# The second turn of x in an even unit: spread at step 5, turned ahead of step 8, copied at step 10

## The reference

```python
e = stack([tbl_f[ids[:, f]] for f in range(39)], axis=1)             # (2048, 39, 16)
z0 = einsum('bid,bjd->bdij', e, e).reshape(B, D, 39 * 39)
cur0 = relu(einsum('bdk,kl->bld', z0, W0))                           # (B, 128, 16)
next_h, direct0 = split(cur0, 2, axis=1)
z1 = einsum('bid,bjd->bdij', e, next_h).reshape(B, D, 39 * 64)
cur1 = relu(einsum('bdk,kl->bld', z1, W1))
z = sum(concatenate([direct0, cur1], axis=1), axis=-1)
h = relu(concatenate([z, dense_ctx], axis=1) @ W_top1 + b_top1)
y = relu(h @ W_top2 + b_top2) @ W_top3
```

## Time and profile before

| | |
|---|---|
| median of 3 runs | 1513.18 us (1512.98 to 1514.53) |
| profiled execution | 1513.26 us |
| its span, first to last instruction | 1511.5 us |
| PE busy | 1442.2 us (95%) |
| DVE busy | 1384.0 us (92%) |
| ACT busy | 822.5 us (54%) |
| POOL busy | 971.7 us (64%) |

### The profile page before, as it was taken

One profiled execution on the slowest core, in us unless ns is written; L12 is line 12 of the kernel. 1 busy time (PEld: TensorE's weight loads), 2 busy tenths in 40 slices (PEclk: granted clock), 3 DMA queues, 4 the chain that ended last, 5 costly groups with the idle time before them and its releaser, 6 DMA issues.

```text
span 1511.5 us, 14915 instructions
## 1 busy us (share of the span) xinstructions
PE 1442.2 (95%) x4458; PEld 785.7 (52%) x4458; DVE 1384.0 (92%) x1244; ACT 822.5 (54%) x897; POOL 971.7 (64%) x604
## 2 busy tenths in 40 slices
PE   4888999999999999999999999999999999999999
PEld 3444545555555554555555555555555555545556
DVE  6778999999999999998999999999999989999993
ACT  1535655655456555545665654556565555655555
POOL 7888888888888778686877868686886830000000
PEclk8999999999999999999999999999999999999999
DMA  5867779888787888877788887878898786778610
GB/s 150 200 154 199 203 190 214 211 186 209 188 205 188 213 198 202 211 184 197 193 199 203 212 204 181 207 190 197 201 207 209 181 207 192 191 194 202 174 35 1
DMA packets 130717, 282.67 MB, mean 187 GB/s; under 512 B 36468, under 2 KB 61700, under 8 KB 130508
## 3 DMA queue, kind: packets, MB, share of 16 engines
q1 hardware_dynamic: 96070, 268.06, 70.4%
q0 software_dynamic: 19200, 4.95, 3.1%
q10 hardware_dynamic: 15366, 8.70, 2.3%
HBM read 273.67 MB, written 7.87 MB: 186 GB/s over the span
## 4 chain that ended last, share of the span: by engine, by line
PE 51%; DVE 26%; issue 14%; POOL 4%; ACT 3%; ACTq 2%; DVEq 0%; DMA 0%
PE psB L533 22%; DVE z L953 12%; PE psA L533 9%; DVE z_lo L962 8%; DVE z_split L953 6%; PE psB L570 4%; PE psB L563 4%; POOL emb L512 4%; PE psB L566 3%; ACTq L751 2%; PE psB L541 1%; ACT z_hi L816 1%; PE psA L553 1%; DVE feat_c L1018 1%; PE psA L563 1%
## 5 line engine op out<-in xcount | busy, mean ns | idle before, releaser
L512 POOL DMA_INDIRECT emb<-in_tbl,ids_all x600 | 971.5, 1619 | 254.5 <-issue 180.1
L533 PE MATMUL psB<-z,w 128*128 128x512 f32 x1544 | 694.0, 594 | 4.1 <-DVE z L953 4.1
L816 ACT ACTIVATE z_hi<-z_split 128x1024 fp32r<-128x1024 f32 x286 | 300.4, 1057 | 465.6 <-DVE z_split L953 410.0
L533 PEld LDWEIGHTS psB<-z,w 128*128 128x128 f32 x1544 | 292.2, 190 | 355.1 <-issue 331.6
L953 DVE TENSOR_TENSOR z<-h_quad,x_lay 128x1024 f32<-128x1024 f32 x354 | 420.2, 1216 | 9.9 <-PE psB L533 4.1
L962 DVE TENSOR_TENSOR z_lo<-z_split,z_hi 128x1024 fp32r<-128x1024 f32 x286 | 349.4, 1222 | 57.7 <-ACT z_hi L816 56.5
L953 DVE TENSOR_TENSOR z_split<-h_quad,x_lay 128x1024 f32<-128x1024 f32 x222 | 267.5, 1217 | 1.7 <-ACT h_quad L769 1.7
L769 ACT ACTIVATE h_quad<-psA 32x1024 f32<-32x1024 f32 x248 | 251.4, 1014 | 3.7
L533 PE MATMUL psA<-z,w 128*128 128x512 f32 x512 | 240.4, 592 | 0.7 <-DVE z L953 0.7
L563 PE MATMUL psB<-z_hi,w_hi 128*128 128x512 f32 x444 | 156.6, 434 | 18.0 <-ACT z_hi L816 18.0
L570 PE MATMUL psB<-z_lo,w_hi 128*128 128x512 f32 x444 | 144.6, 407 | 19.1 <-DVE z_lo L962 17.2
(11 more groups left out here) (121 smaller groups left out, 836.7 us busy)
## 6 DMA issues: line engine op xcount, KB each, us to landing
x_lay<-x_rows SPq DMA_DIRECT2D x1152, 128.0 KB, 7.0
bases<-x_rows SPq DMA_DIRECT2D x62, 468.0 KB
x_more<-x_rows SPq DMA_DIRECT2D x62, 468.0 KB
x_lay<-x_rows SPq DMA_DIRECT2D x64, 256.0 KB, 3.9
x_ring<-x_rows SPq DMA_DIRECT2D x31, 468.0 KB
emb<-in_tbl,ids_all POOLq DMA_INDIRECT x600
x_last<-x_rows SPq DMA_DIRECT2D x64, 128.0 KB, 9.7
x_rows<-x_side ACTq DMA_DIRECT2D x58, 120.0 KB
```

Source lines behind the costliest of these rows:

```text
L512: nc.gpsimd.indirect_dma_start(emb[t % 2][:, f * D:(f + 1) * D], None, tables[f], bass.IndirectOffsetOnAxis(ids_all[:, t, f:f + 1], 0)).th ...
L533: mm = nc.tensor.matmul(ps[:, cs], w[0:k, :], z[WHOLE_NO[place] % NZ][0:k, cs], start=first, stop=last)
L816: nc.scalar.activation(z_hi[n % NS][0:k, 0:cols], z_split[n % NS][0:k, 0:cols], ACT.Copy).then_inc(z_hi_made, 1)
```

## The change

For u = 2, 4, ..., 28 the turn of unit u+3 on PE goes from ahead of step 11 to ahead of step 8. ACT's spread of an odd unit goes from one step ahead of the turn to three, its copy stays two steps behind it: spread at step 5 (was 10), copy and stores at step 10 (were at 13). In the body of u = 0 the turn of unit 3 stays ahead of step 15 and its copy at step 17; its spread goes from step 14 to 12. The first turn of each even body (unit u+2: spread at 0, turn ahead of 2, copy at 4) stays as it is.

```diff
@@ def turns(u):
     if u % 2 or u + 2 >= UNITS:
         return ()
-    return ((u + 2, 9), (u + 3, 15)) if u == 0 else ((u + 2, 2), (u + 3, 11))
+    return ((u + 2, 9), (u + 3, 15)) if u == 0 else ((u + 2, 2), (u + 3, 8))
@@ ACT's body(u)
                 for s in range(STEPS1):
                     for v, t in turns(u):
-                        if s == t - (2 if v % 2 == 0 else 1):
+                        if s == t - (2 if v % 2 == 0 else 3):
                             spread_x(v)
                         if s == t + 2:
                             keep_x(v)
```

## The result

| | before | after |
|---|---|---|
| median | 1513.54 us (1512.98 to 1514.53, 4 runs) | 1469.45 us (1468.99 to 1469.76, 4 runs) |
| ratio | | 0.9708 (95% interval 0.9691 to 0.9725) |
| span of the profiled execution | 1511.5 us | 1467.9 us |

The change makes the kernel 44.1 us faster, 2.9%. The forecast was 1470.6.

What follows compares the result with a forecast made beforehand. PE and DVE, both nearly full and coupled, were taken to bound the kernel, with PE setting the pace. 14 x (2.15 + 0.67 + 0.22) = 42.6 us off 1513.2 gave 1470.6 us, range 1468 to 1484.

Steps and rivals of the forecast that it cites:

- The bottleneck and the stall's cause: PE and DVE nearly full; in even bodies ACT's copy at step 13 awaits PE's turn, delaying `high(13)`: DVE idle 3.15 us.
- 2.15 us for the even body: Half step 12 to splits 13 and 14: PE took 6.09 us, against 3.94 in the odd body; difference 2.15 us gained.
- 0.67 and 0.22 us for the odd body: PE's waits for `z_lo` at step 9 (0.67 us) and step 3 (0.22 us) should both go, through DVE's new lead.
- The thin margins: Odd body: DVE's 1.00 us of new lead exceeds the 0.89 us of waits by 0.11; `z` ring at step 1 leaves 0.14.
- a reserve of 0.11 us in DVE's lead: Odd body: DVE's new lead of 1.00 us against 0.89 us of PE's waits for `z_lo`, 0.11 us to spare.
- the ring: Full `z` buffers at step 1 of the odd body could hold DVE; margin 1.14 us before, 0.14 after: just fits.
- rival 1: Only the even body's stall goes, DVE's lead being lost on the way: 14 x 2.15 = 30.1 us gained, 1483.1 us; 22%.
- The costs taken as nothing: Even body: spread at step 5 (2.2 us cover), turn before step 8 (net 0.01 us), copy at 10 (3.1 us cover): 0.
- Rival 2: A new DVE wait, for `x_lay` or `z_hi` elsewhere, partly replaces the old: 1498 us, range 1488 to 1508; 8%.
- Rival 3: Slower: DMA becomes the bound, stores and gathers delaying SP's loads; at 8 us later, 27 us slower, 1540 us; 4%.
- the reserve of 3.1 us: Step 2 of the odd unit: time left between the `x_lay` load's landing and its use in the new kernel, 3.1 us.
- Rival 4: The change doesn't do what it says: the late `high(13)` has another cause than the copy; 1513 us; 4%.

Runs made afterwards that it cites:

- the full dose: Changed kernel with DVE's product of step 16 done a second time (1024 columns) in the 14 even bodies, into an unread tile: 1485.63 us.

## Why the prediction was right

**The bottleneck and the stall's cause** held as told. The prediction read from rows 3 to 5 that ACT had room on average and none at step 13. Moving the turn (with the spread that it needs) brings all of the gain and moving the spread alone none, so the cause is where the prediction put it: PE's late turn, handed on through ACT's order.

**2.15 us for the even body.** From step 15 of the odd body before it to its own step 15 PE took 723.41 - 679.24 = 44.17 us and takes 703.31 - 661.34 = 41.97: 2.20. Right.

**0.67 and 0.22 us for the odd body.** From there to step 15 of the next odd body PE took 766.73 - 723.41 = 43.32 and takes 745.65 - 703.31 = 42.34: 0.98, where 0.89 was forecast. The sum of a pair was 3.04, its size in the trace 87.50 - 84.31 = 3.19. The term that was somewhat too small is the price of a wait. The next two starts of PE after the waits in rows 6, in the kernel before:

```profile
741.61 1.88 PE L533 MATMUL psA<-z,w 128*128 128x512 f32 x4
...
756.48 1.88 PE L533 MATMUL psA<-z,w 128*128 128x512 f32 x4
```

After 741.03 and 755.90 they come 0.58 us later, where a part without a wait in front takes 0.46: a wait costs PE its gap and some 0.12 us more. Two such waits are 0.24; in the other direction, step 9 still loses 0.57 - 0.46 = 0.11 in the changed kernel, and as much again behind it (735.44 - 734.87 = 0.57). Together 0.89 + 0.24 - 0.22 = 0.91 of the 0.98.

**The thin margins** (a reserve of 0.11 us in DVE's lead, and 0.14 us at the ring) are the point at which rival 1 would have won. That the forecast came out so near is in part luck: the sum left out the price behind each wait (0.24 us too little) and the small wait that stays (0.22 us too much), and the two nearly cancel. The first margin was too hopeful by about 0.2 us: the 0.57 us at 734.87 is a small wait where none was forecast. A wait of that size costs 0.22 us, not the whole term.

**The costs taken as nothing** were nothing. Spread and `relu1` end before `high(7)` with 2.3 us to spare (2.2 forecast); the copy's stores with 2.9 (3.1 forecast). The turn at its new place takes 691.89 - 690.99 = 0.90 together with the split part behind it, the same 0.90 that its neighbour before step 2 took the earlier trace rows. An estimate from the 275 ns that the Trainium skill (TensorE: Matmul & The Clock Gate, Part 4) gives for a transpose, four of them taken serially, would have made it 1.1 us more than the split part; the trace decides for 0.44.

**The rivals.** Rival 1 (1483) is excluded by the measured time and by PE's waits for `z_lo`, 17.2 us before and 0.6 after. The runs with more work on DVE show that the term it leaves out is real: the full dose brings the waits at steps 3 and 9 back and costs 1.16 us a pair, near the 0.89 + 0.24 = 1.13 above. Rival 2 (a new wait in part) isn't in the changed kernel, but it is what happens when the copy is moved instead of the turn: 1487 us. Rival 3 (DMA) didn't come, and the runs with more traffic show how far off it was: with three times 448 KB a body DVE waited for `x_lay` 3.2 us in the whole span. The expectation of 100 us had assumed that 1344 KB make the loads 6.5 us later; they were issued 2.6 us later and took no longer in the median, and the reserve of 3.1 us isn't contradicted. That DMAs of all issuers share 16 engines (DMA: Bandwidth & Descriptors, Issuing engines are not separate DMA queues, of the Trainium skill) was no reason for a loss here: the run with three transfers moved 241 GB/s instead of 206, and its median lies within 2 us of the changed kernel's. Rival 4 is excluded by the run in which only the turn moved.

**What DVE loses, PE pays.** The runs give one relation that the prediction had only for the two kernels. Lost by DVE in each pair of bodies, and the time above the changed kernel divided by 14:

| kernel | DVE loses | cost of a pair |
|---|---|---|
| half multiplication more | 0.6 us (512 columns) | 0.57 us |
| copy behind `high(14)` | 1.05 us | 1.26 us |
| whole multiplication more | 1.14 us | 1.16 us |
| turn ahead of step 10 | 1.41 us | 1.44 us |
| before | 3.15 us | 3.15 us |

The last row is 44.1 / 14. The relation is one to one within about 0.2 us, for losses between the half step of the even body and the first split products of the odd one. It holds although in the changed kernel PE is busy throughout and DVE is not in every pair (82.46 of 84.31 us in the second stretch above).

## What to carry to other kernels

An engine that is half idle can hold two full ones, by one instruction that waits for something late in front of one that is due: look at the order in its queue, and move the producer of what it waits for (here the turn on PE), not the waiting instruction (which, moved alone, met the next tight place here and gave 60% of the gain). When a stall disappears, look for the body behind it too: a lead that one engine gets back pays for waits in places that the change doesn't touch, and the odd body without the copy gave the price beforehand. Where two coupled engines are both nearly full (here 96% or more of two bodies), count what either loses at full price until the trace shows a wait that would take it up.

## What was not expected of the hardware

The busy share of DMA was no measure of the room left. In the changed kernel it was 0.86 at 206 GB/s; with 1344 KB more in each body the same pairs of bodies had 0.92 and 0.89 at 241 GB/s, 17% more bytes for 3 to 7% more share, and bodies no longer. Why it reads so isn't shown by any run here, and the added bytes were stores to DRAM alone.
